# A decoder layer on one core: the adds of neighbouring states on GpSimd given up, TensorE sums every state itself

## The reference, cut to what matters

```python
# u, delta: (2048 tokens, 512 channels); A: (512, 16 states); Bm, Cm: (2048, 16)
def step(h, inp):
    d_t, u_t, b_t, c_t = inp
    dA = jnp.exp(d_t[..., None] * A)
    h = dA * h + (d_t * u_t)[..., None] * b_t[:, None, :]
    y = jnp.einsum('bdn,bn->bd', h, c_t)
    return (h, y)
...
y = selective_scan(u, delta, A, Bm, Cm) + u * D
y = y * jax.nn.silu(z)
```

## Time and profile before

| | us |
|---|---|
| runs | 1878.11, 1881.87, 1881.72 |
| median | 1881.72 |
| span of the profiled execution, first to last instruction | 1872.7 |
| DVE busy in the span | 1081.3 |
| PE busy | 1398.0 |
| POOL busy | 541.5 |
| POOL's 20 adds (L448) | 60.3 |

### The profile page before, as it was taken

One profiled execution on the slowest core, in us unless ns is written; L12 is line 12 of the kernel. 1 busy time (PEld: TensorE's weight loads), 2 busy tenths in 40 slices (PEclk: granted clock), 3 DMA queues, 4 the chain that ended last, 5 costly groups with the idle time before them and its releaser, 6 DMA issues.

```text
span 1872.7 us, 15244 instructions
## 1 busy us (share of the span) xinstructions
PE 1398.0 (75%) x5491; PEld 644.1 (34%) x5491; DVE 1081.3 (58%) x1089; ACT 897.9 (48%) x1136; POOL 541.5 (29%) x182
## 2 busy tenths in 40 slices
PE   6254555668556677466796449999999998889999
PEld 2121122224222243123454222232222323448888
DVE  5999999999999999999608220010100101644001
ACT  4332224344333523343022339989989894563210
POOL 0654636555465555566305200000000000000000
PEclk8676668778778887777888659999999997999999
DMA  5010110111010111011105980000000000010611
GB/s 185 23 45 23 46 45 23 44 45 47 22 45 28 40 46 43 25 45 45 46 0 73 105 86 1 1 1 1 1 0 0 0 0 1 1 45 1 271 44 45
DMA packets 26411, 74.32 MB, mean 40 GB/s; under 512 B 2627, under 2 KB 13123, under 8 KB 23700
## 3 DMA queue, kind: packets, MB, share of 16 engines
q1 hardware_dynamic: 26356, 73.63, 15.2%
HBM read 60.05 MB, written 2.36 MB: 33 GB/s over the span
## 4 chain that ended last, share of the span: by engine, by line
DVE 40%; PE 35%; issue 10%; ACT 8%; DMA 4%; SPq 1%; POOL 1%; DVEq 0%; ACTq 0%; POOLq 0%
DVE arena L885 16%; PE ps L1535 8%; PE ps L1520 8%; DVE arena L895 8%; ACT arena L713 5%; PE ps L1644 3%; DMA arena<-arena 3%; PE ps L1685 3%; DVE arena L875 2%; DVE arena L820 2%; DVE arena L824 2%; PE ps L1673 1%; PE ps L1662 1%; PE ps L1254 1%; SPq L388 1%
## 5 line engine op out<-in xcount | busy, mean ns | idle before, releaser
L442 POOL TENSOR_TENSOR arena<-arena 128x1024 f32<-128x1024 f32 x128 | 408.4, 3192 | 406.2 <-DVE arena L885 307.1
L885 DVE TENSOR_TENSOR_SCAN arena<-arena 128x512 f32<-128x512 f32 x256 | 474.0, 1865 | 2.5 <-POOL arena L442 2.5
L1313 PE MATMUL ps<-arena,ident 128*128 128x512 f32 x432 | 274.2, 776 | 233.8 <-DVE arena L895 122.7
L713 ACT ACTIVATE arena<-ps,bound 128x1024 f32<-128x1024 f32 (+1 forms) x416 | 420.7, 1213 | 26.0 <-PE ps L1520 26.0
L565 ACT ACTIVATE arena<-arena 128x512 f32<-128x512 f32 x256 | 169.5, 713 | 509.4 <-DVE arena L885 429.1
L1520 PE MATMUL ps<-arena 97*128 (+3 forms) x832 | 218.2, 384 | 22.2 <-issue 20.1
L1313 PEld LDWEIGHTS ps<-arena,ident 128*128 128x128 f32 x432 | 95.6, 238 | 387.9 <-DVE arena L895 168.7
L1535 PE MATMUL ps<-arena 128*32 128x512 f32 (+1 forms) x1664 | 222.5, 607 | 1.1 <-ACT arena L713 0.9
L1147 DVE COPY arena<-ps 128x512 f32<-128x512 f32 x16 | 11.1, 691 | 353.6 <-PE ps L1535 353.6
L430 POOL TENSOR_TENSOR rstd<-ve,mhalf 128x4 f32<-128x4 f32 (+3 forms) x18 | 30.7, 1707 | 587.3 <-DVE ve L1172 467.7
L895 DVE TENSOR_TENSOR arena<-arena 128x1024 f32<-128x1024 f32 x128 | 159.6, 1246 | 0.1
(11 more groups left out here) (183 smaller groups left out, 1544.9 us busy)
## 6 DMA issues: line engine op xcount, KB each, us to landing
arena<-bc_scratch SPq DMA_DIRECT2D x64, 512.0 KB, 4.4
arena<-in_mw SPq DMA_DIRECT2D x16, 1024.0 KB, 9.4
arena<-arena SPq DMA_DIRECT2D x48, 128.0 KB, 14.8
arena<-arena SPq DMA_DIRECT2D x12, 400.2 KB, 16.8
arena<-in_w SPq DMA_DIRECT2D x2, 1024.0 KB
out<-xt SPq DMA_DIRECT2D x4, 512.0 KB, 2.9
xt<-in_x SPq DMA_DIRECT2D x1, 1536.0 KB
arena<-in_ctx SPq DMA_DIRECT2D x1, 1200.8 KB, 7.5
```

Source lines behind the costliest of these rows:

```text
L442: pool.tensor_tensor(dbu[:, w % 2], du[:, 2 * p:2 * p + 2], over(bg[:, q % 2, n % BG], 2), ALU.mult).then_inc(S["dbu_ready"], 1)
L713: act.activation(flat(prob[0:n, v % 2, 2 * h:2 * h + 2]), ps[0:n, 2 * (r % 3):2 * (r % 3) + 2, :].rearrange("p a b -> p (a b)"), ACT.Exp, ...
L885: dve.tensor_tensor_scan(state(w)[:, x], da[:, w % AHEAD, x], dbu[:, w % 2, x], carry[:, d, n:n + 1], ALU.mult, ALU.add).then_inc(S["scan_ ...
L1313: last = mm(bank(2 * p + x), ident[:, :], state(2 * j + s)[:, x], start=False, stop=(j >= NP - DP and (j in SUMMED or s == 1)))
```

## The change

The list of pairs that POOL adds becomes empty:

```diff
@@ -53,7 +53,7 @@
 DP = DB // 2
 NU = NS * DP
 NP = NU // 2
-SUMMED = [j for j in range(NP - 1) if j % 3 == 0]
+SUMMED = []
 RING = 3
 AHEAD = 4
 UB = [6, 7, 6, 7]
```

## The result

The changed kernel takes 1836.66 us, the median of 4 runs (1835.72 to 1836.94); the kernel before, with one run more on the same chip, 1880.17 (1878.11 to 1881.87). The ratio is 0.9767, 95% interval 0.9753 to 0.9781: 43.5 us or 2.3% faster. The forecast was 1840.0, range 1831 to 1850.

The account below looks back on a forecast made before the run. DVE's unbroken sequence was taken to bound the scan, stretched by POOL's adds. Removing 20 adds saves 29.5 + 6.3 + 5.9 = 41.7 us: span 1872.7 - 41.7 = 1831.0, plus 9.0 gives 1840.0 us, range 1831 to 1850.

Parts of the forecast that it names:

- The sum, 41.7 us: Scan: time DVE gains from removing 20 POOL adds, 29.5 + 6.3 + 5.9 us.
- The plain steps: Scan steps holding 14 of the adds: 2.11 us each, 29.5 us saved.
- the convolution's: Three scan steps with an add beside the convolution (L824): 1.95 us each, 5.9 us saved.
- The three beside L808: Three scan steps with an add beside the normalisation: 2.1 us each assumed, 6.3 us saved.
- PE's added work costs nothing: Scan: two more matmuls for each of 20 pairs, 35 to 75 us of PE time, charged at 0.
- The tail: Stretch behind the scan: taken as 0, upper bound +7 us, lower bound some 9 us shorter.
- rival 1: Behind the scan, PE at half clock gives back up to 7 us: 1847 to 1852 us; chance 0.10.
- L901 near 866: The gate behind the scan was to come near 866 us instead of 912.
- The 9.0 us between span and run: Whole kernel: median of the runs put 9.0 us above the profiled span, added to 1831.0 to give 1840.0.
- Rival 2: Scan: each add costs DVE its recorded time, 20 x 3.0 = 60 us, giving 1821 us; chance 0.06.
- Rivals 3 and 4: Scan: PE becomes the bound, 1888 us, chance 0.05; DVE's room refilled by other waits, 1880 us, chance 0.04.
- rival 3: Scan steps with feed-forward: PE at half clock becomes the bound, slower than before, 1888 us; chance 0.05.

Follow-up runs that it names:

- 1: Changed kernel with GpSimd's product L442 issued twice in the twenty places where the adds stood: 1877.93 us, kernel before 1877.27.
- 4: Kernel before with eight pairs a chunk added by GpSimd instead of five, 32 adds instead of 20: 1891.60 us.
- the filling: Changed kernel plus four matmuls nobody reads, in PE's wait for the attention's weights behind L1320: 1836.22 us; again 1834.97, unaltered beside it 1832.10.
- 5: Changed kernel with four unread matmuls in PE's pause behind the scan, 1836.22 us; repeated beside the unaltered changed kernel, 1834.97 against 1832.10.

## Why the prediction was right, point by point

- *DVE sets the pace of the scan and POOL stretches it.* Shown: 1 returns the whole cost with PE's work as changed, 4 and the table make it linear.
- *The sum, 41.7 us.* Measured from the first L895 to the last: 41.36. The plain steps gave 2.09 to 2.13 each, the convolution's 1.95, as reckoned. The three beside L808 gave 2.02, not 2.1.
- *PE's added work costs nothing.* Right for the scan: DVE's scans never wait for L1313, and even six times the addition cost only 8.6 us up to the gate. L1313 grew by 33.4 us of busy time.
- *The tail.* Taken at 0; in the two profiles it grew by 3.4 us. L901 waited 1.1 us longer, because the last twelve L1313 took 8.36 us with part of them at the half clock, where before the last eight took 3.70. Even this is not a fixed price of the change: with the same scan, L901 waits 2.35 us in the changed kernel's second profile, and 3.43 and 1.26 in the two with the filling, which stands behind it. The stretch from L901 to the end was 2.3 us longer, but not where the prediction looked: to L1038 it got 1.6 shorter (75.1 to 73.5), and behind L1038 3.9 longer (885.6 to 889.5), for which no cause was found. So rival 1 had the right sign; its mechanism gave 1.1 us of its 7, and its other half, L1320 at half clock, did not come. Nor had PE worked without a break in the 20 us before the gate: it stood 1.54 and 1.57 us before its last two groups of L1313.
- *L901 near 866 in the prediction's last part* was my slip: 912.0 - 41.7 is 870.3; measured 871.8.
- *The 9.0 us between span and run* were mistaken. Of the later runs the span is on record too, and in every one of these two kernels the time lies 2.1 to 2.2 us above it. The profiled run of before was thus about 1874.8, a quick one, not 1881.7. By its own time the sum reads 1874.8 - 41.7 = 1833.1, and with 1.1 + 2.3 us of the tail, and the 0.3 by which the steps gave less, mostly those beside L808, 1836.8: measured 1836.9 in the run that was profiled. The forecast of 1840.0 was off by only 3.3 us because a base 6.9 too high partly made up for a tail costed too low. That part is luck, and so is the nearness of 41.7 to the 43.5 between the medians: the two profiled spans differ by 37.9 (1872.7 and 1834.8). What stands on its own is the 41.36 of the scan.
- *Rival 2* (recorded durations, 60 us) failed: of an add's 3.25 us 1.1 are its own wait. *Rivals 3 and 4* did not appear. But the reason given against rival 3, that PE is granted the full clock when it works without breaks, does not hold: in the earlier trace rows it is busy for 18.45 of 19 us at 0.50, and in the changed kernel for 19.31 of 20 at 0.53.

## What to carry to other kernels

Where VectorE sets the pace, a GpSimd instruction that reads SBUF is not free work beside it: look in the timeline for a tiny VectorE instruction with a duration of microseconds that ends together with a GpSimd instruction, and price the GpSimd instruction by the distance between two like VectorE steps, with it and without it, not by the waits (there are none) nor by its record. If VectorE could do the same work in less time than it is shut out, move it there; here that was worth 96 to 102 us, more than twice the change under study. And before explaining some 10 us, see which of the two clocks TensorE had in the stages behind: the profiles of two kernels that differed by a memset differed by that much there (951.7 and 963.0 us), and the changed kernel's own runs by up to 17.7.

## What the runs showed of the hardware that was not expected

- A GpSimd memset of 128 x 1024 float32, 0.95 us, ran beside a two-operand VectorE instruction without stretching it; a product of the same size in the same twenty places (1) shut DVE out for 1.96 to 2.13 us in each.
- Which instruction is held up depends on what DVE starts next, and it need not have two SBUF operands: the copy L875, 128 x 2, with one operand, was held up like the scans. The sums L906, which take one operand from PSUM, ran at 0.67 to 0.68 us beside L442 in all six places of the kernel before where the two overlap.
- Behind the scan a pause of PE of 3.1 to 4.0 us was followed by the half clock for 23.9 to 27.3 us in all six profiles that have it, although PE was then busy nearly all the time (in the changed kernel 19.31 of 20 us; there all of L1409 from 886 us on, and L1339 in part, which took 16.86 us where it takes 14.00 with the filling). After a pause of 1.5 to 1.7 us (four profiles) or none (four) the full clock stayed there. From L901 to L1038 this makes 73.5 to 75.1 us in the six against 62.7 to 64.4 in the eight. In two of the four profiles with the filling the clock fell 47 and 56 us after the first L1409, for 23.9 and 6.8 us, with no pause above 0.78 us before it (5).
- The same program's runs spread by 1.2 us in one session and by 17.7 in another (the changed kernel, 4 and 6 runs). Where in a run the clock is lost is not settled.
